# Two routed passes over 48 tiles each become one pass over 80 common tiles, with the shared units inside it

## The chip, the core and the metric

The kernel runs on one core of a Trainium2 chip. The metric is the device time of one execution in microseconds. The engines are PE (TensorE), DVE (VectorE), ACT (ScalarE), POOL (GpSimd) and SP (SyncE, which here only issues DMAs); each runs its own list of instructions in order and waits on semaphores that the others raise. The program writes every engine's list itself, so the order of the lists is the schedule.

## What is computed

Two batches of 1024 tokens with 256 features pass through two decoder layers. All but the last block (linear attention, two cross attentions, a spline block, causal attention) is untouched. The last block is a mixture of 16 experts, of which each token takes 4, plus one shared expert that every token takes:

```python
scores = jax.nn.sigmoid(x @ gate_w.T)                  # x: 2048 tokens x 256
topk_w, topk_ids = jax.lax.top_k(scores, K)            # K = 4 of E = 16
topk_w = topk_w / topk_w.sum(-1, keepdims=True)
comb = zeros((T, E)).at[arange(T)[:, None], topk_ids].add(topk_w)
g, u = einsum('th,ehi->tei', x, Wg), einsum('th,ehi->tei', x, Wu)
eo = einsum('tei,eih->teh', silu(g) * u, Wd)
routed = einsum('teh,te->th', eo, comb)
shared = silu(x @ sg) * (x @ su) @ sd
x = x + shared + routed
```

## The kernel before

Each token-expert pair (1024 x 4 per batch) gets a slot in a DRAM table of rows, `rows_by_slot`, one table per batch. Slots come in tiles of 128 rows, each tile of one expert only. An expert with n tokens takes n/128 tiles, rounded up; with 4096 pairs and 16 experts that can reach 48 tiles for one batch, and the program always works through all 48, whether they hold rows or not. Two tiles make a unit: 24 routed units per batch (`ROUTED_UNITS`), and 4 shared units of 2 tiles of tokens per batch. In all there are 56 units.

The steps of the last block, by batch b:

- `context_out(b, "e")`: 4 projections on PE (L720), each added to X by DVE (L1523) with the statistics of the layer norm behind it; then the norm and its transposes (L1408, L620).
- `route(b)`: gate scores on PE (L1006), then on DVE the choice of 4 experts (L1854 to L1877), each pair's place among its expert's rows from small matmuls on PE (L1015 to L1021), the number of tiles per expert and the first tile of each (L1893 to L1903), and each pair's slot (L1904 to L1917, which raises `slots_done`). POOL then waits for `slots_done` and issues the **dispatch**: 32 indirect DMAs (L2151), each of which scatters 128 rows into the table. DVE also works out the expert of each tile (L1921 to L1930, `experts_done`).
- `experts(b)`: a pipeline over units. In the turn of unit x, PE transposes the rows of unit x (L1041), multiplies those of unit x-1 by its experts' gate and up weights (L1055), transposes the hidden values of x-2 (L1067) and multiplies those of x-3 by the down weights (L1074). ACT copies and applies silu (L1353, L1358, L1366), DVE multiplies and copies (L1942, L1948), adds a shared unit's output to X (L1952), and for a routed unit finds the token of each row (L1960 to L1967). SP loads the rows of a unit (L2318) into one of 3 buffers; before the first unit of a batch it waits for all 32 dispatch DMAs of that batch.
- `results(b)`: POOL scatters each routed unit's output to `outs_by_token`, 2 indirect DMAs a unit (L2166), from 11 buffers.
- `combine(b)`: SP waits for all results of the batch and loads them back tile by tile (L2334, 512 KB each, 4 buffers for batch 0 and 8 for batch 1); DVE adds 4 weighted rows per token to X (L1981, 4 instructions a tile, 8 tiles). Stores of X follow (L2410).

`in_order` (L561) sets the order of all engines: every engine passes through the same nest of generators, and `next(other)` puts one step of a side job between two turns of the main job. Before the change `experts(0)` starts with the 4 shared units of batch 0 and then its 24 routed units, with `context_out(1, "e")` and `route(1)` beside it at two steps a turn; `experts(1)` starts with its routed units and ends with the 4 shared ones, with `combine(0)` beside it from turn 12. A turn's own work stands in the lists ahead of the side steps of the same turn.

## Time and profile before

| | us |
|---|---|
| median of 3 runs | 1254.06 |
| fastest, slowest of 3 | 1252.6, 1254.81 |
| span of the profiled execution | 1256.2 |
| PE busy | 1066.6 (85%) |
| DVE busy | 803.1 (64%) |
| ACT busy | 578.9 (46%) |
| POOL busy | 393.0 (31%) |

The profiled execution is 2.1 us longer than the median. Busy shares are averages over very different stages; the last block fills about the last 235 us, and what sets its pace has to be read there, from the timelines of its engines.

### The profile page before, as it was taken

The page shows a single profiled execution, that of the slowest core. Times are in us where ns is not written, and L with a number is a line of the kernel's source. Part 1 is how long each engine was busy: PE and PEld are TensorE (multiplying, and loading weights), DVE is VectorE, ACT ScalarE, POOL GpSimd, SP SyncE. Part 2 cuts the span into 40 slices and gives each one's busy share as a digit, 9 for nine tenths or more (in the row PEclk, how much of TensorE's full clock was granted, in tenths as well). Part 3 has the DMA queues.
Part 4 walks back from the last instruction along what each step waited for, and adds up shares of the span by engine and source line. Part 5 has one row for each costly group of instructions (what it writes and reads, how often), then busy time and mean ns, then how long its engine had stood idle before and what let it go on. Part 6 is the DMA issues. An engine that isn't in the chain of part 4 may idle for free.

```text
span 1256.2 us, 19418 instructions
## 1 busy us (share of the span) xinstructions
PE 1066.6 (85%) x6344; PEld 647.4 (52%) x6344; DVE 803.1 (64%) x2216; ACT 578.9 (46%) x1185; POOL 393.0 (31%) x458
## 2 busy tenths in 40 slices
PE   4688888997768885989999998988997888989993
PEld 2244554575534563324444453436555457878873
DVE  4867666658465558485577676717767954633576
ACT  2333026732367632367666554674443533434430
POOL 3231023320175430044100020003422730777771
PEclk9999889997679996599999999999997998999997
DMA  7145847672001460304133320007000211555665
GB/s 198 67 101 114 114 64 253 205 113 31 1 0 38 94 109 0 51 1 102 51 52 52 51 44 8 3 1 214 1 1 1 96 69 40 164 170 160 203 196 202
DMA packets 63201, 107.90 MB, mean 86 GB/s; under 512 B 13433, under 2 KB 35291, under 8 KB 62816
## 3 DMA queue, kind: packets, MB, share of 16 engines
q1 hardware_dynamic: 55104, 76.61, 27.6%
q0 software_dynamic: 7680, 17.07, 3.7%
q10 hardware_dynamic: 320, 12.98, 3.2%
q8 instruction: 55, 0.90, 0.3%
q14 instruction: 42, 0.34, 0.1%
HBM read 74.75 MB, written 48.89 MB: 98 GB/s over the span
## 4 chain that ended last, share of the span: by engine, by line
PE 52%; DVE 24%; ACT 8%; issue 7%; DMA 4%; POOL 3%; SPq 1%; DVEq 0%; ACTq 0%; POOLq 0%
PE psum L1055 7%; PE psum L934 5%; PE psum L720 4%; PE psum L904 4%; DVE mx L1796 4%; PE psum L956 4%; PE psum L1074 3%; PE psum L832 3%; PE psum L805 2%; PE psum L816 2%; DVE small L1581 2%; PE psum L620 2%; DVE work L1596 2%; PE psum L862 2%; DVE X L1981 1%
## 5 line engine op out<-in xcount | busy, mean ns | idle before, releaser
L1796 DVE TENSOR_REDUCE mx<-psum 128x1 f32<-128x512 f32 (+3 forms) x384 | 195.7, 551 | 89.5 <-PE psum L904 46.5
L1321 ACT ACTIVATE work<-psum 128x512 f32<-128x512 f32 (+1 forms) x192 | 92.5, 527 | 60.9 <-PE psum L959 41.0
L904 PE MATMUL psum<-stack_area 96*128 96x512 bf16 (+3 forms) x288 | 98.5, 353 | 25.1 <-DVE mx L1796 23.8
L2098 POOL TENSOR_TENSOR work<-work,small 128x308 f32<-128x308 f32 x107 | 74.7, 703 | 114.0 <-DVE small L1599 114.0
L805 PE MATMUL psum<-area 128*128 128x308 f32 x256 | 96.5, 461 | 14.2 <-DVE work L1596 11.5
L1321 ACT ACTIVATE HT<-psum 128x384 f32<-128x384 f32 (+2 forms) x192 | 81.1, 465 | 49.0 <-PE psum L959 31.6
L956 PE MATMUL psum<-stack_area 98*128 98x512 bf16 (+3 forms) x288 | 93.5, 337 | 7.9 <-ACT work L1321 2.8
L2006 POOL TENSOR_SCALAR rstd<-mv 128x4 f32<-128x4 f32 (+1 forms) x26 | 6.6, 255 | 298.2 <-DVE mv L1418 221.5
L1055 PE MATMUL psum<-area,work 128*128 x384 | 94.2, 390 | 5.7 <-ACT work L1353 5.7
L816 PE MATMUL psum<-const_tile,work 128*77 128x128 f32 x512 | 81.4, 285 | 15.1 <-ACT stack_area L1233 9.4
L1581 DVE TENSOR_REDUCE small<-psum 128x4 f32<-128x308 f32 x128 | 59.3, 463 | 51.9 <-PE psum L805 25.5
L816 PEld LDWEIGHTS psum<-const_tile,work 128*77 128x77 f32 x512 | 62.8, 152 | 52.8 <-POOL work L2098 31.0
L1942 DVE TENSOR_TENSOR work<-work,psum 128x256 f32<-128x256 f32 x56 | 23.5, 419 | 92.8 <-ACT work L1358 92.8
L620 PE MATMUL psum<-const_tile,H 128*128 128x128 f32 x224 | 44.0, 333 | 44.9 <-DVE H L1408 34.2
L1055 PEld LDWEIGHTS psum<-area,work 128*128 128x128 f32 x384 | 71.5, 196 | 14.5 <-issue 6.2
L1225 ACT ACTIVATE work<-work,rowany 128x308 f32<-128x308 f32 x64 | 35.3, 552 | 82.2 <-DVE work L1596 82.1
L904 PEld LDWEIGHTS psum<-stack_area 96*128 96x128 bf16 x288 | 28.7, 100 | 85.7 <-DVE mx L1796 47.0
L2166 POOL DMA_INDIRECT outs_by_token<-stack_area,area x66 | 65.4, 991 | 21.6 <-issue 18.6
L1233 ACT COPY stack_area<-psum 77x512 f32<-77x512 f32 x128 | 71.5, 566 | 1.3 <-PE psum L816 1.3
L2151 POOL DMA_INDIRECT rows_by_slot<-area x64 | 61.8, 965 | 22.1 <-issue 18.9
L805 PEld LDWEIGHTS psum<-area 128*128 128x128 f32 x256 | 42.3, 198 | 44.5 <-issue 21.8
L620 PEld LDWEIGHTS psum<-const_tile,H 128*128 128x128 f32 x224 | 30.4, 169 | 60.1 <-issue 28.7
(264 smaller groups left out, 2442.4 us busy)
## 6 DMA issues: line engine op xcount, KB each, us to landing
rows_by_slot<-in_unused_rows ACTq DMA_DIRECT2D x2, 6336.0 KB, 32.8
W<-rows_by_slot SPq DMA_DIRECT2D x48, 264.0 KB, 3.0
stack_area<-parts_a0q SPq DMA_DIRECT2D x24, 128.0 KB, 4.2
stack_area<-parts_a0k SPq DMA_DIRECT2D x24, 128.0 KB, 6.7
stack_area<-parts_a1q SPq DMA_DIRECT2D x24, 128.0 KB, 4.5
stack_area<-parts_a1k SPq DMA_DIRECT2D x24, 128.0 KB, 6.9
H<-outs_by_token SPq DMA_DIRECT2D x6, 512.0 KB, 4.1
area<-outs_by_token SPq DMA_DIRECT2D x6, 512.0 KB, 5.8
```

What stands on the lines that cost most here:

```text
L620: done = pe.transpose(u.bank(k)[:, q * P:(q + 1) * P], src[:, t, c * P:(c + 1) * P], ident)
L805: done = pe.matmul(s, queries[:, g // 2 if masked else g, t * P:(t + 1) * P], keys[:, g, :, :].rearrange("p j k -> p (j k)"), start=True, ...
L816: done = pe.transpose(turned.bank(i)[0:CTX, j * P:(j + 1) * P], work[i % 6][:, j * CTX:(j + 1) * CTX], ident)
L904: done = pe.matmul(u.bank(k)[:, 0:cols], stack["q"][0:KSTACK, j, t * P:(t + 1) * P], stack["k"][0:KSTACK, j, half * SPAN:half * SPAN + col ...
L956: done = pe.matmul(u.bank(k)[:, 0:cols], stack["k"][0:KSTACK + 2, j, kb * P:(kb + 1) * P], stack["q"][0:KSTACK + 2, j, c * SPAN + off:(c + ...
L1055: done = pe.matmul(u_g.bank(g)[:, q * D:(q + 1) * D], lhs, w, start=q == 0 and c == 0, stop=c == DC - 1, skip_group_check=True)
L1233: act.copy(pt[group % 2][0:CTX, :, q * P:(q + 1) * P], turned.bank(i)[0:CTX, :].rearrange("p (j n) -> p j n", j=HPG)).then_inc(*turned.emp ...
L1321: act.activation(p[:, 0:cols], u.bank(k)[:, 0:cols], ACT.Exp).then_inc(*u.empties(k))
L1581: dve.tensor_reduce(mx, s3, AX.X, ALU.max).then_inc(*steps.up())
L1796: dve.tensor_reduce(mxt[n % 2][:, j, t, half:half + 1], u.bank(k)[:, 0:cols], AX.X, ALU.max).then_inc(*u.empties(k))
L2098: pool.tensor_tensor(ex3, ex3, small[:, of_i + 4:of_i + 8].unsqueeze(2).to_broadcast([P, HPG, CTX]), ALU.mult).then_inc(ctx_prob, 1)
L2166: pool.indirect_dma_start(outs_dram[b], bass.IndirectOffsetOnAxis(m.out_row[:, tile:tile + 1], 0), unit_out[slot][:, q * D:(q + 1) * D], N ...
```

## The change

The tables of the two batches become one of 80 tiles (40 routed units). Batch 0 first gets the full tiles of each of its experts, rounded down instead of up. Then come 16 tiles, one for each expert, that take what is left of that expert from batch 0 and are filled up from batch 1; the rest of batch 1 follows. All engines now run one `experts()` of 48 units: 8 routed units (the first 16 tiles are always full tiles of batch 0), then the 8 shared units of both batches, then the other 32 routed units. SP waits for the dispatch of batch 0 before routed unit 0 and for that of batch 1 before routed unit 8. `combine(0)` now starts at turn 41 and needs the first 24 units' results; `combine(1)` needs all 40.

```diff
-DISPATCH_START, COMBINE_START, COMBINE_LAG = 13, 12, 2
+COMBINE_START, COMBINE_LAG = 41, 2
-ROUTED_UNITS = 24
+ROUTED_UNITS = 40
+EARLY_UNITS, FIRST_BATCH_UNITS = 8, 24
+ROUTE_RATES = (4, 2, 2, 2, 3, 3, 3, 3, 4)
+RESULT_RATES, RESULTS_FROM = {4: 1, 5: 1, 6: 1, 7: 1, 16: 2, 17: 2}, 20
...
             drain(other)
-            other, results = chain(e["context_out"](1, "e"), e["route"](1)), e["results"](0)
-            for n, _ in enumerate(e["experts"](0)):
-                next(other, None)
-                next(other, None)
-                if FIRST_ROUTED[0] + UNIT_STEPS <= n < DISPATCH_START:
-                    next(results, None)
-            drain(other)
-            results, other = chain(results, e["results"](1)), e["combine"](0)
-            for n, _ in enumerate(e["experts"](1)):
-                next(results, None)
-                if n % 2 == 0:
+            other, results, returned = chain(e["context_out"](1, "e"), e["route"](1)), e["results"](), e["combine"](0)
+            for n, _ in enumerate(e["experts"]()):
+                for _ in range(ROUTE_RATES[min(n, len(ROUTE_RATES) - 1)]):
+                    next(other, None)
+                for _ in range(RESULT_RATES.get(n, int(n >= RESULTS_FROM))):
                     next(results, None)
                 if n >= COMBINE_START:
-                    next(other, None)
+                    next(returned, None)
+            drain(other)
             drain(results)
-            drain(other)
+            drain(returned)
             drain(e["combine"](1))
...
# SP, experts
-                        if routed == 0:
-                            sp.wait_ge(dispatched[b].sem, 16 * TILES * TOPK)
+                        if routed == 0:
+                            sp.wait_ge(dispatched[0].sem, 16 * TILES * TOPK)
+                        if routed == EARLY_UNITS:
+                            sp.wait_ge(dispatched[1].sem, 16 * TILES * TOPK)
...
# DVE, route: the slots
-                dve.tensor_tensor(m.end, m.first, m.tiles, ALU.add).then_inc(*steps.up())
-                dve.scalar_tensor_tensor(m.slot, m.first.unsqueeze(1).to_broadcast([P, TILES, EXPERTS]), float(P),
-                                         u.bank(1)[:, 0:P].rearrange("p (t e) -> p t e", t=TILES), ALU.mult, ALU.add).then_inc(*u.empties(1))
+                if b == 0:
...
+                else:
+                    dve.tensor_tensor(m.end, m.first, m.tiles, ALU.add).then_inc(*steps.up())
+                    dve.tensor_scalar(m.base, const("iota16"), full_tiles, float(P), ALU.add, ALU.mult).then_inc(*steps.up())
+                    dve.tensor_scalar(m.bound, m0.left, -1.0, float(P), ALU.mult, ALU.add)
+                    dve.tensor_tensor(m.jump, m.first, const("iota16"), ALU.subtract).then_inc(*steps.up())
+                    dve.wait_ge(*steps.now())
+                    dve.tensor_tensor(m.base, m.base, m0.left, ALU.add)
+                    dve.tensor_scalar(m.end, m.end, full_tiles, float(EXPERTS), ALU.add, ALU.add)
+                    dve.tensor_scalar(m.jump, m.jump, float(EXPERTS - 1), float(P), ALU.add, ALU.mult).then_inc(*steps.up())
+                dve.wait_ge(*steps.now())
+                dve.tensor_tensor(m.past, place, m.bound.unsqueeze(1).to_broadcast(by_e), ALU.is_ge).then_inc(*steps.up())
+                dve.tensor_tensor(m.slot, place, m.base.unsqueeze(1).to_broadcast(by_e), ALU.add).then_inc(*u.empties(1))
+                dve.wait_ge(*steps.now())
+                dve.tensor_tensor(m.past, m.past, m.jump.unsqueeze(1).to_broadcast(by_e), ALU.mult).then_inc(*steps.up())
+                dve.wait_ge(*steps.now())
                 dve.wait_ge(*u.empty(1))
+                dve.tensor_tensor(m.slot, m.slot, m.past, ALU.add).then_inc(*steps.up())
...
# SP, combine
-                    sp.wait_ge(landing.sem, 16 * UNIT_TILES * results_in(slot, b))
+                    sp.wait_ge(landing.sem, 16 * UNIT_TILES * results_in(slot, ROUTED_UNITS if b else FIRST_BATCH_UNITS))
```

Where the lists change, line numbers of the changed kernel are some 10 to 55 higher: L1046 is the old L1041, L1063 L1055, L730 L720, L2206 L2151, L2220 L2166.

**POOL, around the dispatch of batch 1.** `rows_by_slot` rows are the dispatch, `outs_by_token` rows the results. Before:

```order
L2166 DMA outs_by_token<-work,area 4096x256 x6
L2166 DMA outs_by_token<-stack_area,area 4096x256 x2
L2151 DMA rows_by_slot<-area 6144x264 x2
L2166 DMA outs_by_token<-stack_area,area 4096x256 x2
L2151 DMA rows_by_slot<-area 6144x264 x2
L2166 DMA outs_by_token<-stack_area,area 4096x256 x2
L2151 DMA rows_by_slot<-area 6144x264 x28
L2166 DMA outs_by_token<-stack_area,area 4096x256 x10
```

and now:

```order
L2220 DMA outs_by_token<-work,area 8192x256 x6
L2220 DMA outs_by_token<-stack_area,area 8192x256 x2
L2206 DMA rows_by_slot<-area 10240x264 x32
L2220 DMA outs_by_token<-stack_area,area 8192x256 x14
L2220 DMA outs_by_token<-work,area 8192x256 x6
```

The first 8 result DMAs stay ahead of the dispatch, the 4 that stood inside it are behind it, and the dispatch is one row of 32.

**PE, the first turns of the experts' pipeline.** `bank` semaphores are those of PSUM, `unit0_landed` says that the rows of a routed unit are in SBUF. Before:

```order
L720 MATMUL psum<-W,H 128x256 [waits landed_wx,bank7_emptied,bank5_emptied,bank6_emptied,bank4_emptied,landed_moe]
L720 MATMUL psum<-W,H 128x256 x3
L720 MATMUL psum<-W,H 128x256 [waits bank7_emptied]
L720 MATMUL psum<-W,H 128x256 x3
L1055 MATMUL psum<-area,HT 128x256 [waits bank2_emptied]
L1055 MATMUL psum<-area,HT 128x256 x3
L720 MATMUL psum<-W,H 128x256 [waits bank7_emptied,bank4_emptied,bank5_emptied]
L720 MATMUL psum<-W,H 128x256 x3
L720 MATMUL psum<-W,H 128x256 [waits bank7_emptied]
L720 MATMUL psum<-W,H 128x256 x3
```

and now:

```order
L1046 MATMUL psum<-const_tile,W 128x128 [waits bank0_emptied,unit0_landed,landed_moe]
L1046 MATMUL psum<-const_tile,W 128x128 x3
L1069 TENSOR_LOAD area [waits experts_done]
L1069 ISA x2
L1069 TENSOR_LOAD area
L1069 ISA x2
L730 MATMUL psum<-W,H 128x256 [waits bank4_emptied,bank7_emptied,bank5_emptied,landed_wx]
L730 MATMUL psum<-W,H 128x256 x3
L730 MATMUL psum<-W,H 128x256 [waits bank7_emptied]
L730 MATMUL psum<-W,H 128x256 x3
L730 MATMUL psum<-W,H 128x256 [waits bank7_emptied,bank4_emptied,bank5_emptied]
L730 MATMUL psum<-W,H 128x256 x3
```

The transposes of routed unit 0 stand first, and the four projections of batch 1 (L730) follow in a block, all in one PSUM bank, where before a shared unit's products (L1055) stood between them.

**DVE, the slots of batch 1**, from the sum of an expert's first tile and its tiles to the product that spreads the slots. Before, down to `slots_done`:

```order
L1903 TENSOR_TENSOR area<-area 128x16
L1904 SCALAR_TENSOR_TENSOR area<-area,psum 128x128
L1907 TENSOR_TENSOR H<-area 128x512
L1910 TENSOR_REDUCE area<-H 128x32
L1912 CAST area<-area 128x32
L1914 TENSOR_SCALAR area<-area 128x32
L1915 TENSOR_SCALAR area<-area 128x32
L1917 SCALAR_TENSOR_TENSOR area<-area 128x32
```

and now, as far as that product (the six rows behind it are as before):

```order
L1925 TENSOR_TENSOR area<-area 128x16
L1926 TENSOR_SCALAR area<-const_tile,area 128x16
L1927 TENSOR_SCALAR area<-area 128x16
L1928 TENSOR_TENSOR area<-area,const_tile 128x16
L1930 TENSOR_TENSOR area<-area 128x16
L1931 TENSOR_SCALAR area<-area 128x16
L1932 TENSOR_SCALAR area<-area 128x16
L1934 TENSOR_TENSOR H<-psum,area 128x128
L1935 TENSOR_TENSOR area<-psum,area 128x128
L1937 TENSOR_TENSOR H<-H,area 128x128
L1940 TENSOR_TENSOR area<-area,H 128x128
L1942 TENSOR_TENSOR H<-area 128x512
```

Two rows ahead of the product have become eleven.

## Rows read from the trace of the kernel before

**Rows 1.** The page, chain of work that ended last, shares of the span

```profile
PE 52%; DVE 24%; ACT 8%; issue 7%; DMA 4%; POOL 3%; SPq 1%; DVEq 0%; ACTq 0%; POOLq 0%
```

**Rows 2.** Timeline of PE: start us, us, engine, line, operation, [idle before]

```profile
1021.67 1.99 PE L720 MATMUL psum<-W,H 128*128 128x256 f32 x8
1024.51 1.99 PE L720 MATMUL psum<-W,H 128*128 128x256 f32 x8 [0.85 <-DVE X L1523]
...
1050.06 5.25 PE L1006 MATMUL psum<-gate_weights,HT 128*128 128x16 f32 x32 [0.72 <-issue]
...
1073.74 0.60 PE L1041 MATMUL psum<-const_tile,W 128*128 128x128 f32 x4
...
1119.24 0.60 PE L1041 MATMUL psum<-const_tile,W 128*128 128x128 f32 x4
```

**Rows 3.** Timeline of PE, around its long wait

```profile
1128.84 3.78 PE L1055 MATMUL psum<-area,work 128*128 x8 [5.75 <-ACT work L1353]
...
1132.83 1.55 PE L1074 MATMUL psum<-stack_area,work 128*128 x4
```

**Rows 4.** Timeline of PE, last routed unit and last shared unit

```profile
1217.69 0.60 PE L1041 MATMUL psum<-const_tile,W 128*128 128x128 f32 x4
...
1220.94 1.89 PE L1055 MATMUL psum<-area,work 128*128 x8
...
1228.51 1.03 PE L1074 MATMUL psum<-stack_area,work 128*128 x4
...
1232.18 1.89 PE L1055 MATMUL psum<-area,HT 128*128 128x256 f32 x8
...
1235.67 1.89 PE L1074 MATMUL psum<-area,work 128*128 128x256 f32 x8
```

**Rows 5.** Timeline of POOL, dispatch of batch 0, then of batch 1

```profile
975.36 1.25 POOL L2151 DMA_INDIRECT rows_by_slot<-area  x1 [2.90 <-DVE area L1917]
...
1014.86 0.96 POOL L2151 DMA_INDIRECT rows_by_slot<-area  x1 [0.30 <-issue]
...
1078.13 0.96 POOL L2151 DMA_INDIRECT rows_by_slot<-area  x1 [0.30 <-issue]
...
1122.56 0.96 POOL L2151 DMA_INDIRECT rows_by_slot<-area  x1 [0.30 <-issue]
```

**Rows 6.** Timeline of DVE, route of batch 1: its first operation, and its slots

```profile
1061.69 0.22 DVE L1854 TENSOR_SCALAR area<-area 128x128 f32<-128x128 f32 x1
...
1071.39 0.28 DVE L1893 TENSOR_TENSOR H<-psum,const_tile 128x128 f32<-128x128 f32 x1
1071.71 0.29 DVE L1896 TENSOR_REDUCE area<-H 128x16 f32<-128x128 f32 x1
...
1076.97 0.19 DVE L1917 SCALAR_TENSOR_TENSOR area<-area 128x32 int32<-128x32 int32 x1
```

**Rows 7.** Timeline of SP, DMA issues: first rows loaded, first results returned

```profile
1018.15 154.88 SPq L2318 DMA_DIRECT2D W<-rows_by_slot  x37
...
1234.49 0.80 SPq L2334 DMA_DIRECT2D H<-outs_by_token  x2
```

**Rows 8.** DMA issues from 1017 to 1035 us: KB each, median us to landing

```profile
W<-rows_by_slot SPq DMA_DIRECT2D x3, 264.0 KB, 3.3
```

**Rows 9.** Busy us by stretch: PE PEld DVE ACT POOL, clock, DMA share, GB/s

```profile
974.40:1015.90 41.50, 36.31 (x183) 18.79 (x181) 38.89 (x113) 22.51 (x45) 31.03 (x32) 1.00 0.28 102
1078.10:1123.60 45.50, 44.99 (x250) 39.11 (x248) 20.26 (x85) 18.06 (x38) 34.72 (x36) 1.00 0.61 189
...
1053.00:1056.00 3.00, 3.00 (x15) 3.00 (x16) 0.00 (x0) 0.28 (x1) 0.00 (x0) 0.50 0.00 0
```

**Rows 10.** Waits from 1026 to 1256 us: total us, times, longest

```profile
PE psum L1041 <- DMA W<-rows_by_slot: 2.7, 4, 1.5
```

**Rows 11.** Timelines of POOL and DVE, last results and last combine

```profile
1232.21 0.97 POOL L2166 DMA_INDIRECT outs_by_token<-stack_area,area  x1 [0.30 <-issue]
...
1238.21 4.00 DVE L1981 SCALAR_TENSOR_TENSOR X<-H,area,X 128x256 f32<-128x256 f32 x8
```

More of the change, by code:

```diff
@@ L343, in routing_memory @@
             m.slot_tile = take(TILES * TOPK, I32)
-            m.slot_f, m.row_f = take(TILES * TOPK), take(ROUTED_UNITS * UNIT_TILES)
-            m.tiles, m.first, m.end = [take(EXPERTS) for _ in range(3)]
-            m.expert = take(ROUTED_UNITS * UNIT_TILES)
-            m.offset = take(ROUTED_UNITS * UNIT_TILES, I32)
-            m.out_row = take(ROUTED_UNITS * UNIT_TILES, I32)
+            m.slot_f = take(TILES * TOPK)
+            m.tiles, m.first, m.end, m.left, m.base, m.bound, m.jump = [take(EXPERTS) for _ in range(7)]
+            if b == 0:
+                m.expert, m.offset = take(ROUTED_TILES), take(ROUTED_TILES, I32)
+            else:
+                m.row_f, m.out_row = take(ROUTED_TILES), take(ROUTED_TILES, I32)
             m.is_k = take(TILES * TOPK * EXPERTS).rearrange("p (t k e) -> p t k e", t=TILES, k=TOPK)
@@ L1052, in experts @@
                                 else:
-                                    t = UNIT_TILES * (g - FIRST_SHARED[b]) + q
+                                    t = UNIT_TILES * pair + q
                                     lhs, w = HT[b][:, c, t * P:(t + 1) * P], wgu_shared[c]
-                                done = pe.matmul(u_g.bank(g)[:, q * D:(q + 1) * D], lhs, w, start=q == 0 and c == 0, stop=c == DC - 1,
+                                done = pe.matmul(u_gu.bank(g)[:, q * D:(q + 1) * D], lhs, w, start=q == 0 and c == 0, stop=c == DC - 1,
@@ L1351, in experts @@
                         if routed >= 2:
-                            act.wait_ge(*u_g.full(x - 2))
-                        act.copy(rows_t[routed % 2].rearrange("p s c n -> p (s c n)"), u_x.bank(routed)).then_inc(*u_x.empties(routed))
+                            act.wait_ge(*u_gu.full(unit_of(routed - 2)))
+                        act.copy(rows_t[routed % 2].rearrange("p s c n -> p (s c n)"), u_rows.bank(routed)).then_inc(*u_rows.empties(routed))
                     if 0 <= g < UNITS:
-                        act.wait_ge(*u_g.full(g))
+                        act.wait_ge(*u_gu.full(g))
@@ L1356, in experts @@
                         if g >= 2:
-                            act.wait_ge(*u_hidden[b].full(g - 2))
-                        act.activation(hidden[g % 2], u_g.bank(g).rearrange("p (s n) -> p s n", s=UNIT_TILES)[:, :, 0:INNER],
+                            act.wait_ge(*u_hidden.full(g - 2))
+                        act.activation(hidden[g % 2], u_gu.bank(g).rearrange("p (s n) -> p s n", s=UNIT_TILES)[:, :, 0:INNER],
                                        ACT.Silu).then_inc(silu_done, 1)
-                    if is_routed(b, d):
-                        routed = d - FIRST_ROUTED[b]
-                        slot, use = out_slot(b, routed)
-                        act.wait_ge(*u_d.full(d))
+                    if d >= 0 and (routed := routed_in(d)) is not None:
+                        slot, use = out_slot(routed)
+                        act.wait_ge(*u_down.full(d))
@@ L1907, in route @@
+                dve.wait_ge(*steps.now())
                 dve.tensor_tensor(m.of_k, m.is_k, m.slot.unsqueeze(2).to_broadcast(wide), ALU.mult).then_inc(*steps.up())
```

271 lines of the change are left out of this document (153 added, 118 removed).

## The prediction

> **What bounds the kernel now.** I read the chain that ended last first: 52% of the span is PE's own work and 24% DVE's [rows 1]. The change touches only the last block, so the timelines of its engines decide. PE is the pacemaker there. Between 1073.74 and 1119.24 us lie 14 routed turns, 3.25 us each [rows 2]; from 1220.94 to 1232.18 lie 4 turns without row transposes, 2.81 us each [rows 4]. The difference, 0.44, is one unit's row transposes. POOL is the second queue to watch: each indirect DMA takes 0.96 us and the next starts 0.3 later, so a dispatch of 32 takes 40.5 us from the first start (975.36) to the last end (1015.82), and every row of it has to be in DRAM before SP may load a unit [rows 5, 7]. Before, the dispatch of batch 1 (1078.13 to 1123.52) ran beside the 24 routed units of batch 0, so PE had work. It was longer than 40.5 only because 4 result DMAs stood in it. Its price was one wait of 5.75 us, since result buffers ran out behind it [rows 3].
>
> **The change, part by part.**
>
> *Units.* 56 turns become 48, all eight of them routed: 8 x 3.25 = 26.0 us less PE work. The number is fixed by the program, not by the data. The second start of the pipeline goes too. Whether this reaches the end depends on whether PE has work at every moment, so I walk through the new order.
>
> *Start.* The route of batch 0 gets longer on DVE: about eight more small operations at 0.19 us or less each, some of them side by side, and two more dependent ones on 128 columns, 0.28 us plus 0.04 [rows 6]: 1.8 us until its slots are done. Its tile table has 32 instead of 48 tiles, which gives some 0.7 back later, too late for the dispatch. DVE is the full engine there, 38.9 of 41.5 us busy [rows 9], so the context stage ends 1.1 to 1.8 later than 1021.67 [rows 2]. The dispatch of batch 0 ends 1.8 later as well; SP issued its first load 2.33 us after the dispatch ended, and the load takes 3.3 [rows 7, 8]: 1018.15 + 1.8 + 3.3 = 1023.3. That was covered by shared units before, and is now the first thing PE waits for. I take 1023.3, 1.6 later.
>
> *To the gate products.* By the end of L1006 at 1055.3 [rows 2], PE had done 5 products, 4 hidden transposes, 3 down products and 2 row transposes of units. In the new order it is 4, 3, 2 and 5. That is 3 x 0.44 more and 2.81 less, so 1.5 less. The four projections now stand in a block in one bank, and each waits 0.85 for DVE's sum [rows 2], one such wait more: +0.9. So the gate products end at 1055.3 + 1.6 - 1.5 + 0.9 = 1056.3. They ran partly at 1.2 GHz before (clock 0.50, [rows 9]); I leave that as it is.
>
> *To the slots of batch 1.* Before, DVE's first route operation came 6.4 us behind them (1061.69, [rows 6]), now without a shared unit's sum (0.6): 1062.1. From there to the end of L1917 it took 15.5 [rows 6], of which I count 4 turns of unit work at 1.5 and 0.4 idle, so 9.1 are the route's own. Now: own 9.1 + 1.8 = 10.9, 2 turns in between instead of 4 (three route steps a turn), 3.0. But the chain now meets PE twice. PE stands at the position matmuls until the choice is made, and DVE's next turn needs the product of a unit that stands behind them: 3.5 us, in which DVE has only 0.9 to do, so +2.6. PE waits some 4.5 us there, and may fall to 1.2 GHz again, which costs 0 to 2; I take 1. Slots done: 1062.1 + 10.9 + 3.0 + 2.6 + 1.0 = 1079.6, against 1077.2 before. The faster rates are eaten up by having fewer turns to hide in. Bounds: 1075 (no half clock, no meeting) and 1083.
>
> *To routed unit 8.* POOL starts 0.97 later (1076.97 + 0.19 to 1078.13, [rows 5, 6]), at 1080.6; its first 8 result DMAs are done by then. Dispatch 40.4, SP 2.33, load 3.3: the rows of unit 8 are there at **1126.6**. PE has only the end of units 6 and 7 and the 8 shared units meanwhile: from 1079.6 on about seven turns of 2.81, so it arrives at about 1099 and **waits 27 us**. This is where the 26 us go. In other words: the 8 shared units are worth 22.5 us, the dispatch with its landing 46.
>
> *From there to the last product.* After its 5.75 us wait, PE worked at 1.2 GHz: the product took 3.78 instead of 1.89, the down product 1.55 instead of 1.03 [rows 3, 4], 2.4 us in all. I take the same. Then 31 turns of 3.25 = 100.8 to the row transposes of the last unit, 3.25 to its product, and 5.4 from that to the end of the last down product (1232.18 to 1237.56, [rows 4]). `combine(0)` falls in the last ten turns; its 512 KB loads held PE's row transposes for 2.7 us in four waits [rows 10], which I take over (bounds 0 and 6, since DVE's 2 us per combined tile now also stands ahead of the last hidden copies). Last product: 1126.6 + 2.4 + 100.8 + 8.6 + 2.7 = 1241.1.
>
> *The tail.* Before, the last routed output left PE at 1229.54 (1228.51 + 1.03, [rows 4]), and four shared units covered what follows. Nothing does now: ACT's copy and the last two result DMAs 3.64 (to 1233.18, [rows 11]), SP's first load 1.31 (1234.49, [rows 7]), the load at most 3.72 (to 1238.21), four rows of 4.00 on DVE that follow 3.92 apart, 15.7 [rows 11], and 2.2 for the last store to the span's end at 1256.2. Together 26.6, against 18.6 from the last PE work to the end before: 8 us exposed. POOL's backlog, which ran to 1222 before, is gone but wasn't late at the end.
>
> *Sum*: 1241.1 + 26.6 = 1267.7, against 1256.2: +11.5. Taken over to the median, 1254.06 + 11.5 = **1265.6 us**.
>
> **A rule beside a row.** The dispatch of batch 0 was issued while DVE was 94% busy, that of batch 1 with DVE at 20.3 of 45.5 us [rows 9], and both go at the same 1.27 us per DMA [rows 5]. The new type casts and table operations of batch 1 stand right behind its slots, so beside the dispatch, some 3.3 us of DVE work in SBUF. If POOL stood still for all of it, the time would be 1269; that is a rival below. The Trainium skill ("SBUF — State Buffer", section "SBUF: two separate sides") says that POOL can't write the descriptors of a DMA that it issues while DVE makes a 32-bit copy inside SBUF, since both need one shared port. By that rule that rival would hold; the rows speak against it.
>
> **Rivals.**
> 1. *Not slower: the dispatch is covered.* If the rows of unit 8 land before PE asks for them, 27 and 2.4 us go: 1236. Every us that the slots come earlier is worth one us until then; it breaks even with before when the slots are done at 1068, 11.5 us earlier than I work out. For it: the route gets three steps a turn instead of two, and the removed work is real. Against it: the gate products end no earlier, the route's own DVE work alone is 10.9 us, and 1056.3 + 10.9 is already 1067. Full cover 3%, enough of it for faster 6%.
> 2. *No difference.* Slots at 1075, no half clock behind the long wait, no contention with `combine(0)`: 1267.7 - 4.6 - 2.4 - 2.7 = 1258, a median of 1256. 9%.
> 3. *Still slower.* Half clock in both waits, slots at 1083, and 6 us around `combine(0)`: 1267.7 + 3.4 + 3.3 = 1274, a median of 1272. 15%, the 1269 of POOL standing still (3%) among it.
> 4. *The forecast*, 1259 to 1270: 67%.
>
> **How the numbers follow.** A difference under 0.2%, 2.5 us, is no change. Faster 0.09, the same 0.09, slower 0.82. The range, 1255 to 1273, reaches from the lower bounds of the unknown terms to their upper ones, and leaves out most of rival 1 and the far end of rival 3.
>
> **What the profile would show.** PE's timeline has one idle stretch of 20 to 33 us ahead of an L1046, ended by the DMA of rows, just behind eight shared turns; SP's wait there names the dispatch. The first L2206 of batch 1 starts at 1077 to 1084 and the 32 of them take 40.4. Turns behind it are 3.25 us. The last product of PE ends 26 to 27 us ahead of the end. I am wrong if DVE finishes the slots ten us earlier than 1079.6, if the indirect DMAs go faster than 1.27 us each, or if the tail is much shorter than 26 us.

## The result, and the profile after

| | before | after |
|---|---|---|
| median | 1253.64 us, 4 runs | 1269.49 us, 4 runs |
| fastest, slowest | 1252.6, 1254.81 | 1267.27, 1276.06 |
| ratio, 95% interval | | 1.014, 1.0102 to 1.0178 |
| span of the profiled execution | 1256.2 | 1266.9 |
| PE busy | 1066.6 | 1038.8 |

The changed kernel is slower by 15.9 us in the medians, with 28 us less work on PE. The prediction was 1265.6, 11.5 slower.

PE, start us, us, operation and the idle time before it, from the first routed unit to the last product:

```profile
1017.70 0.66 PE L1046 MATMUL psum<-const_tile,W 128*128 128x128 f32 x4
1019.29 1.97 PE L730 MATMUL psum<-W,H 128*128 128x256 f32 x8 [0.94 <-ACT H L1248]
...
1052.63 3.62 PE L1063 MATMUL psum<-area,work 128*128 x8
...
1064.80 0.29 PE L1025 MATMUL psum<-area 128*128 128x128 bf16 x1 [3.94 <-DVE area L1881]
...
1066.41 3.62 PE L1063 MATMUL psum<-area,work 128*128 x8
...
1123.99 1.11 PE L1046 MATMUL psum<-const_tile,W 128*128 128x128 f32 x4 [25.80 <-DMA W<-rows_by_slot]
1124.90 3.61 PE L1063 MATMUL psum<-area,HT 128*128 128x256 f32 x8
...
1129.43 0.60 PE L1046 MATMUL psum<-const_tile,W 128*128 128x128 f32 x4
...
1132.68 0.60 PE L1046 MATMUL psum<-const_tile,W 128*128 128x128 f32 x4
...
1237.73 1.12 PE L1082 MATMUL psum<-stack_area,work 128*128 x4 [0.93 <-DVE work L2004]
```

The first row transposes start with hardly a pause behind the context stage: the rows of batch 0 landed at about 1017.5, just as PE got there. Between 1052 and 1070 two products take 3.62 us, twice the 1.89 of [rows 4]. The granted clock is at its lower level there, 1.2 GHz, behind the small matrices of the gate scores (from 1047.27) and behind the wait of 3.94 us, as windows over these two stretches show (columns as in [rows 9], the clock is the 0.50):

```profile
1050.00:1056.00 6.00, 6.00 (x21) 5.22 (x22) 0.00 (x0) 2.15 (x3) 0.00 (x0) 0.50 0.07 25
1065.00:1070.00 5.00, 5.00 (x29) 4.17 (x28) 0.35 (x2) 0.59 (x1) 0.00 (x0) 0.50 0.07 26
```

Then the row that decides: **25.80 us idle, ended by the DMA of rows**, and the turn behind it mostly at 1.2 GHz once more (5.44 us from 1123.99 to 1129.43 instead of 3.25). After that the turns stand 3.25 apart, as in [rows 2]. The chain of work that ended last shows the same in shares, against [rows 1]:

```profile
PE 49%; DVE 25%; ACT 8%; issue 8%; POOL 5%; DMA 4%; SPq 1%; DVEq 0%; POOLq 0%; ACTq 0%
```

PE went from 52% to 49%, POOL from 3% to 5%: the dispatch now lies on the path. POOL's timeline has both dispatches and the last results, to be laid beside [rows 5, 11]:

```profile
972.16 1.25 POOL L2206 DMA_INDIRECT rows_by_slot<-area  x1 [4.51 <-DVE area L1952]
...
1078.50 1.76 POOL L2206 DMA_INDIRECT rows_by_slot<-area  x1 [13.99 <-DVE area L1952]
1080.56 0.96 POOL L2206 DMA_INDIRECT rows_by_slot<-area  x1 [0.30 <-issue]
...
1118.50 0.96 POOL L2206 DMA_INDIRECT rows_by_slot<-area  x1 [0.30 <-issue]
...
1238.64 1.23 POOL L2220 DMA_INDIRECT outs_by_token<-stack_area,area  x1 [0.30 <-issue]
1240.18 1.13 POOL L2220 DMA_INDIRECT outs_by_token<-stack_area,area  x1 [0.30 <-issue]
1241.61 0.97 POOL L2220 DMA_INDIRECT outs_by_token<-stack_area,area  x1 [0.31 <-issue]
1242.89 0.97 POOL L2220 DMA_INDIRECT outs_by_token<-stack_area,area  x1 [0.30 <-issue]
```

The dispatch of batch 1 takes 41.0 us (1078.50 to 1119.46), one DMA every 1.27, and PE's wait ends 4.5 behind it. At the end four result DMAs stand close together, and the last is issued at 1243.86, 5.0 us after PE's last product (1238.85). DVE: the first route operation of batch 1, the hidden product that it waits for, the last operation of the slots, then combine(1):

```profile
1058.05 0.22 DVE L1858 TENSOR_SCALAR area<-area 128x128 f32<-128x128 f32 x1
...
1070.48 0.42 DVE L1998 TENSOR_TENSOR work<-work,psum 128x256 f32<-128x256 f32 x1 [5.10 <-ACT work L1363]
...
1077.53 0.19 DVE L1952 SCALAR_TENSOR_TENSOR area<-area 128x32 int32<-128x32 int32 x1
...
1248.88 4.01 DVE L2036 SCALAR_TENSOR_TENSOR X<-H,area,X 128x256 f32<-128x256 f32 x8 [7.38 <-DMA H<-outs_by_token]
...
1260.64 4.00 DVE L2036 SCALAR_TENSOR_TENSOR X<-W,area,X 128x256 f32<-128x256 f32 x8
```

SP, DMA issues, the first rows loaded and the first results of batch 1 returned, against [rows 7]:

```profile
1014.71 187.58 SPq L2370 DMA_DIRECT2D W<-rows_by_slot  x34
...
1245.38 0.80 SPq L2388 DMA_DIRECT2D H<-outs_by_token  x2
```

**Where the 15.9 us are.** The profiled spans differ by 10.7 only, and the reason lies ahead of the change. Windows of the kernel before in two stretches that it doesn't touch (columns as in [rows 9]):

```profile
240.00:360.00 120.00, 102.24 (x743) 68.23 (x736) 71.62 (x183) 48.62 (x95) 26.50 (x34) 0.83 0.29 49
360.00:600.00 240.00, 195.70 (x989) 103.87 (x988) 153.43 (x403) 131.32 (x272) 86.03 (x113) 0.86 0.27 53
```

and of the changed one:

```profile
240.00:360.00 120.00, 100.34 (x750) 67.42 (x750) 73.24 (x188) 53.27 (x102) 30.92 (x39) 0.89 0.29 49
360.00:600.00 240.00, 198.75 (x1008) 104.36 (x1008) 154.97 (x406) 131.02 (x273) 83.02 (x109) 0.86 0.28 55
```

In the first stretch the granted clock was 0.83 before and 0.89 after; in the second it was 0.86 in both. The last norm ahead of the dispatch of batch 0 started at 949.91 before and at 944.42 after, 5.5 us earlier. From that norm to the end it is 306.3 and 322.5 us, **16.2 more**, and that agrees with the medians. In all profiles of this study the first dispatch DMA starts somewhere from 966.6 to 978.2 (a last one, on another chip, apart), though no experiment edits anything ahead of it (the change itself puts a longer route of batch 0 there). So the experiments are read by the distance from that DMA to the end of the span, beside the medians: 280.8 us before, 294.7 after (plus 2.3 for the longer route ahead of it).

### The profile page after: what moved, and what is told of

It reads as the page before. It is cut to its first block, busy times and chain, and to the rows that moved or that the text cites. A ratio compares the mean times of both kernels' runs of the same rounds, so it can differ in the third digit from the quotient of the medians.

```text
span 1266.9 us, 18868 instructions
## 1 busy us (share of the span) xinstructions
PE 1038.8 (82%) x6200; PEld 623.9 (49%) x6200; DVE 796.0 (63%) x2191; ACT 567.1 (45%) x1161; POOL 378.0 (30%) x442
## 4 chain that ended last, share of the span: by engine, by line
PE 49%; DVE 25%; ACT 8%; issue 8%; POOL 5%; DMA 4%; SPq 1%; DVEq 0%; POOLq 0%; ACTq 0%
PE psum L1063 5%; PE psum L944 5%; PE psum L730 4%; PE psum L914 4%; DVE mx L1800 4%; PE psum L966 4%; PE psum L842 3%; PE psum L815 2%; POOL rows_by_slot L2206 2%; PE psum L826 2%; DVE small L1585 2%; PE psum L630 2%; PE psum L1082 2%; DVE work L1600 2%; DVE X L2036 1%
## 5 line engine op out<-in xcount | busy, mean ns | idle before, releaser
L1585 DVE TENSOR_REDUCE small<-psum 128x4 f32<-128x308 f32 x128 | 59.3, 463 | 51.1 <-PE psum L815 25.8
L1998 DVE TENSOR_TENSOR work<-work,psum 128x256 f32<-128x256 f32 x48 | 20.2, 421 | 109.0 <-ACT work L1363 109.0
L1063 PE MATMUL psum<-area,work 128*128 x320 | 79.2, 392 | 0.0
L2206 POOL DMA_INDIRECT rows_by_slot<-area x64 | 63.0, 984 | 37.4 <-issue 18.9
L2220 POOL DMA_INDIRECT outs_by_token<-stack_area,area x56 | 55.4, 989 | 41.8 <-ACT stack_area L1370 20.1
L1063 PEld LDWEIGHTS psum<-area,work 128*128 128x128 f32 x320 | 60.1, 198 | 7.1
L1600 DVE TENSOR_TENSOR work<-psum,small 128x308 f32<-128x308 f32 x128 | 60.0, 469 | 0.3
```

The costliest lines, as they stand in the source:

```text
L1063: done = pe.matmul(u_gu.bank(g)[:, q * D:(q + 1) * D], lhs, w, start=q == 0 and c == 0, stop=c == DC - 1, skip_group_check=True)
L1585: dve.tensor_reduce(mx, s3, AX.X, ALU.max).then_inc(*steps.up())
L1600: dve.tensor_tensor(ex3, s3, mx.unsqueeze(2).to_broadcast([P, HPG, CTX]), ALU.subtract).then_inc(*score.empties(n))
L2206: pool.indirect_dma_start(rows_dram, bass.IndirectOffsetOnAxis(m.slot_k[:, at:at + 1], 0), m.rows[:, t, :], None).then_inc(*dispatched[b]. ...
```

## The experiments

The theory: the dispatch of batch 1, which ran beside 24 routed units before, now runs beside eight shared ones, and the path to the end is route, dispatch, unit 8, 32 units, tail. The rival theories, named in the prediction or suggested by the result: the longer DVE route is the cause by itself; turns with less in them shift the dispatch; another queue (results, buffers, tables) is just as late; the tail is what costs.

| run | median us | ratio to before, 95% | PE's wait for rows of batch 1 | first dispatch DMA to end |
|---|---|---|---|---|
| before | 1253.3 to 1254.2 | | 0 | 280.8 |
| changed | 1269.49 | 1.014 (1.010 to 1.018) | 25.8 | 294.7 |
| changed, again | 1270.08 | 1.016 (1.009 to 1.022) | 25.5 | 296.0 |
| e1 half dispatch | 1249.01 | 0.997 (0.994 to 1.000) | 5.4 | 274.3 |
| e2 12 early units | 1254.59 | 1.004 (1.001 to 1.007) | 12.9 | 282.4 |
| e3 route first | 1248.12 | 0.996 (0.994 to 0.999) | 1.0 | 273.2 |
| e3 again | 1245.38 | 0.993 (0.990 to 0.996) | 1.3 | 274.0 |
| e4 shared split | 1269.97 | 1.014 (1.010 to 1.019) | 37.1 | 298.6 |
| e5 before, route first | 1257.71 | 1.005 (1.002 to 1.008) | 0 | 285.9 |
| e6 = e2 + e3 + e4 | 1240.15 | 0.989 (0.986 to 0.992) | 0 | 264.7 |
| e7 = e1 + e3 | 1246.91 | 0.995 (0.991 to 0.999) | 0 | 272.8 |
| e8 route in turn 4 | 1259.24 | 1.003 (1.001 to 1.006) | 13.0 | 281.9 |
| e9 e3, part of combine(1) on POOL | 1252.34 | 0.998 (0.996 to 1.001) | 1.3 | 276.6 |

**The changed kernel again.**

> The changed kernel itself again, beside the other three on the same chip, since its first runs lay between 1267.3 and 1276.1. My theory: 1268 to 1270, with 25.8 us of wait before unit 8 as in its first profile, since what varies lies in the stages ahead of the last block. Rival, the wait itself varies by several us with the time at which the dispatch lands: the end would vary with it.

1270.1, with the wait at 25.5. The two profiles of this one program differ by 4.4 us in when the first dispatch DMA starts (972.16 and 967.76), by 1.3 in what follows it, and by 0.3 in the wait. What varies lies ahead of the last block, as expected.

**Is the wait the dispatch?** Half of the DMAs of batch 1 are left out, and with them the rows of 512 tokens:

```diff
                 for t in range(TILES):
                     for k in range(TOPK):
+                        if b and t >= TILES // 2:
+                            yield
+                            continue
...
-                            sp.wait_ge(dispatched[1].sem, 16 * TILES * TOPK)
+                            sp.wait_ge(dispatched[1].sem, 16 * TILES * TOPK // 2)
...
-                    sp.dma_start(returned_rows[b][t % slots], by_token[t]).then_inc(*returned_landed[t % slots].up())
+                    sp.dma_start(returned_rows[b][t % slots], by_token[t % (TILES // 2) if b else t]).then_inc(*returned_landed[t % slots].up())
```

> The changed kernel, but only 16 of the 32 dispatch DMAs of batch 1 are issued (those of its first 512 tokens), and SP waits for 16. The rows of the other 512 tokens are left out, and combine(1) adds the routed sums of the first 512 tokens to them in their place; all turns, loads and results stay as many. My theory: the 25.8 us that PE stands before unit 8 are the dispatch, and nothing else is late there. 16 x 1.27 = 20.3 us less, so a wait of 5.5 us, and the end comes 20.3 us earlier, up to 22.7 if the half clock behind the wait goes too: a median of 1247 to 1249, against 1269.5 of the changed kernel. Rival A, something else is late behind the dispatch (results, buffers, tables of experts): the wait is replaced by another one and the gain is below 10 us, 1260 or more. Rival B, the time is in the longer route of DVE and not in the dispatch: hardly any gain.

The row transposes of unit 8, on PE:

```profile
1104.88 1.11 PE L1046 MATMUL psum<-const_tile,W 128*128 128x128 f32 x4 [5.43 <-DMA W<-rows_by_slot]
```

The median fell by 20.5, for 20.3 us of DMAs taken away. Nothing else was late behind the dispatch.

**Does work ahead of the wait cost anything?**

```diff
-EARLY_UNITS, FIRST_BATCH_UNITS = 8, 24
+EARLY_UNITS, FIRST_BATCH_UNITS = 12, 24
```

> The changed kernel with 12 early routed units instead of 8 (with this input batch 0 has 26 full tiles, so 24 tiles can go ahead; the program's guarantee is only 16). The same 48 turns, but four routed turns move from behind PE's long wait to ahead of it. My theory: the wait ends when the dispatch of batch 1 has landed, whatever PE does before; four turns of 3.25 us fill 13.0 of its 25.8 us, 12.8 remain, and the end comes 13.0 us earlier, 1256.5. Rival A, the turns only shift the dispatch (its route steps stand between turns, PE and DVE are full): wait and end stay within 3 us, 1267 or more. Rival B, the wait isn't a landing time but a chain through the results' buffers: then four more results ahead lengthen it, 1270 or more.

```profile
1119.26 1.12 PE L1046 MATMUL psum<-const_tile,W 128*128 128x128 f32 x4 [12.88 <-DMA W<-rows_by_slot]
```

Wait 12.9, as worked out, and the distance to the end 13 us shorter than the mean of the changed kernel's two profiles (295.4). Four turns moved into the gap were free. With rival A the dispatch would have moved; its first DMA comes 106.7 us after that of batch 0, 106.3 in the changed kernel.

**What is a turn inside the route worth?** e3 lists all side steps right behind the first turn, e8 lists those from the second half of the norm on in turn 4:

```diff
-ROUTE_RATES = (4, 2, 2, 2, 3, 3, 3, 3, 4)
+ROUTE_RATES = (64,)
```

```diff
-ROUTE_RATES = (4, 2, 2, 2, 3, 3, 3, 3, 4)
+ROUTE_RATES = (4, 2, 2, 2, 64)
```

> The changed kernel with all side steps (projections, norm and route of batch 1, dispatch issues) in the lists directly behind the first turn of the experts, not 4, 2, 2, 2, 3 ... a turn. No work is removed. My theory: the path is route, dispatch, unit 8, and turns that stand inside the route lengthen it one to one. Without them slots are done at about 1060 instead of 1077.7, the rows of unit 8 are there at about 1107 instead of 1123; the 7 other early turns and the 8 shared ones (45 to 48 us) just fill the 46 us of the dispatch, so the wait is under 3 us, and the end comes 15 to 18 us earlier: a median of 1252 to 1255. PE stands instead some 10 to 15 us in pieces inside the route, which costs nothing, as it is the path itself. Rival A, the idle time in the route is as dear as the wait it saves: 1266 or more. Rival B, more is won, since DVE and ACT finish the route faster than I count (slots before 1055): below 1250.

> The changed kernel with side steps 4, 2, 2, 2 in the first turns as it has them, and all others (the rest of the norm, gate products, route, dispatch) in turn 4, where it spreads them over turns 4 to 8 and beyond. It lies between the changed kernel (slots done 13.5 us... 19.7 us from the first route operation) and e3 (12.4 us). My theory: three unit turns leave the path (one ahead of the first route operation, two behind it). The first route operation comes 5.8 us earlier, as it no longer stands behind the turn after the gate products, and the slots 7.3 us more: 13 us earlier, the wait before unit 8 shrinks from 25.8 to about 13 us, and the time is 1270 - 13 = 1257. Rival, what e3 won lies in the first turns (projections and norm without unit work between them): then this is worth little, 1265 or more.

e3, DVE's first and last operation up to the slots, and PE's waits:

```profile
1045.56 0.23 DVE L1858 TENSOR_SCALAR area<-area 128x128 f32<-128x128 f32 x1 [12.01 <-ACT area L1348]
...
1057.74 0.19 DVE L1952 SCALAR_TENSOR_TENSOR area<-area 128x32 int32<-128x32 int32 x1
...
1051.11 0.29 PE L1025 MATMUL psum<-area 128*128 128x128 bf16 x1 [5.90 <-DVE area L1881]
...
1061.81 0.44 PE L1075 MATMUL psum<-const_tile,work 128*128 128x128 f32 x2 [3.52 <-DVE work L1998]
...
1103.65 0.66 PE L1046 MATMUL psum<-const_tile,W 128*128 128x128 f32 x4 [0.98 <-DMA W<-rows_by_slot]
```

The slots are done at 1057.93, 86.7 us after the first dispatch DMA (105.6 in the changed kernel), 12.4 us after the first route operation (19.7). PE stands 5.90 us inside the route, 3.52 right behind its slots, and 0.98 for the rows. The end comes 21.8 us earlier by the distance (mean of two profiles each): 19.4 from the earlier rows, the rest since the turn behind the wait now runs at full clock. Rival A, that idle time in the route is as dear, is out. e8 lies between, wait 12.99:

```profile
1113.09 1.11 PE L1046 MATMUL psum<-const_tile,W 128*128 128x128 f32 x4 [12.99 <-DMA W<-rows_by_slot]
```

Its time is 2.2 above the 1257 expected, its distance 13.5 under the changed kernel's. With the slots done 105.6, 92.8 and 86.7 us behind the first dispatch DMA (changed, e8, e3), the end is 295.4, 281.9 and 273.6 behind it: 12.7 us of route are 13.5 of time, and the next 6.1 are 8.3, with the half clock behind the wait, 2.2 us, gone at the last step. In this range a us of route is a us of time.

e3 ran a second time, as the pair of e9 (below):

> e3 itself again, as the pair of e9 on the same chip, and for a closer interval against the kernel before. My theory: 1248, a ratio of 0.996 as in its first runs. Rival: its first runs were lucky by some us, and it is the same as the kernel before, 1254.

1245.4 and 0.993 (0.990 to 0.996): the gain over the kernel before is real.

**Is route first simply better?** The same edit in the kernel before:

```diff
             for n, _ in enumerate(e["experts"](0)):
-                next(other, None)
-                next(other, None)
+                drain(other)
```

> The kernel before the change (two tables, 56 units), with the same edit as e3: all side steps of batch 1 directly behind the first turn. My theory: an earlier route is worth something only where PE waits for the dispatch. Here it never does, so 20 us earlier slots bring nothing; PE stands about 12 us more inside the route (17.7 us of gaps there in e3, 5.5 in the kernel before), with no wait later that it pays back, except the 5.75 us for result buffers and the 2.4 us of half clock behind it, which go since POOL has its dispatch done earlier. Sum +4: 1258. Rival A, route first is simply the better order: 1235 to 1245. Rival B, the gaps in the route are hidden by other work: 1246 to 1250.

1257.7: slower by 0.5%, by 5.1 us in the distance. Where routed units cover the dispatch, PE's gaps inside the route are paid and nothing is won.

**Is the dispatch dear where PE doesn't wait for it?** e3 with half a dispatch:

> e3 and e1 together: side steps first, and only 16 of the 32 dispatch DMAs of batch 1 (the rows of its last 512 tokens are left out, and the sums of the first 512 are added to them). My theory: in e3 PE is at the balance, 1 us of wait is left before unit 8, so 20 us less dispatch are worth 1 us: 1247. In e1 the same cut was worth 20.5 us. Rival, POOL's dispatch is dear in itself, also where PE doesn't wait for it (by the traffic or the late results): 1240 or less.

PE no longer waits for rows of batch 1 at all, yet the cut that was worth 20.5 us is now worth nothing clear of noise: 0.8 us by the distance, and a ratio of 0.995 that lies between the 0.996 and 0.993 of e3. The dispatch has no price of its own; e3 is at the balance, with 1.0 to 1.3 us of wait left.

**The tail against the wait.** Four shared units go behind the last routed one:

```diff
+        MIDDLE = SHARED_UNITS
...
-            return n - SHARED if EARLY_UNITS + SHARED <= n < UNITS else None
+            return n - MIDDLE if EARLY_UNITS + MIDDLE <= n < ROUTED_UNITS + MIDDLE else None
...
+            if ROUTED_UNITS + MIDDLE <= n < UNITS:
+                return divmod(n - ROUTED_UNITS, SHARED_UNITS)
...
```

> The changed kernel with the four shared units of batch 1 behind the last routed unit, where they stood before the change, and only the four of batch 0 in the middle. My theory: the four turns (11.2 us) come out of the cover of the dispatch, so PE waits 37.0 us instead of 25.8, and they cover the tail, which from PE's last down product shrinks from 28.05 to the 18.6 us of the kernel before, 9.4 less. Sum +1.8: 1271. Rival A, the tail isn't shortened (the results and the combine are late for another reason): +11.2, 1281. Rival B, the wait in the middle doesn't grow, since the dispatch starts earlier with less DVE and PE work ahead of it: 1260.

The first row is PE, the others are DVE in the tail, the last tiles of combine(0) and the first of combine(1):

```profile
1118.25 1.12 PE L1049 MATMUL psum<-const_tile,W 128*128 128x128 f32 x4 [37.10 <-DMA W<-rows_by_slot]
...
1245.21 2.04 DVE L2039 SCALAR_TENSOR_TENSOR X<-area,X 128x256 f32<-128x256 f32 x4
1247.17 4.00 DVE L2039 SCALAR_TENSOR_TENSOR X<-H,area,X 128x256 f32<-128x256 f32 x8
```

The wait grew by 11.3 to 37.1, and the time stayed: what the middle lost, the tail gave back. The distance is 3.2 longer, where 1.8 were expected; two profiles of one program differ by 1.3, so that excess says little. But the DVE rows show that the tail gave back less than it could: DVE goes from combine(0) to combine(1) without a gap, though POOL's last result DMA had been issued by 1236.88. In place of the results DVE itself is now late in the tail.

**All together.**

> The edits of e2, e3 and e4 together: 12 early units (for this input only), side steps first, four shared units in the middle and four at the end. My theory: PE has 12 routed and 4 shared turns, 50 us, for the 46 us from the slots to the rows of unit 12, so the wait stays near 0, as in e3, and now the four last shared turns cover 9.4 us of the tail: 1248.1 - 9.4 = 1238.7. Rival, the gains don't add, since the early units hold DVE or POOL up (results of 12 units behind the dispatch, 11 buffers): a new wait of 5 us or more behind the dispatch, 1244 or more.

1240.15, and 8.9 us under e3 by the distance, where 9.4 were expected. The gains add, since each fills another gap. It is faster than the kernel before by 13 us and than the changed one by 30, but it needs 24 full tiles in batch 0 (this input has 26; only 16 are sure). **e3 has no such condition and is faster than both kernels too**, 0.993 and 0.996 of the kernel before. In e6 DVE again has no gap between combine(0) and combine(1) (DVE rows), long after POOL's last result:

```profile
1221.53 2.04 DVE L2039 SCALAR_TENSOR_TENSOR X<-area,X 128x256 f32<-128x256 f32 x4
1223.48 4.00 DVE L2039 SCALAR_TENSOR_TENSOR X<-H,area,X 128x256 f32<-128x256 f32 x8
...
1212.24 0.98 POOL L2223 DMA_INDIRECT outs_by_token<-stack_area,area  x1 [0.30 <-issue]
```

So the last run moves combine(0) ahead:

```diff
-COMBINE_START, COMBINE_LAG = 41, 2
+COMBINE_START, COMBINE_LAG = 37, 2
```

> e6 (12 early units for this input, side steps first, four shared units at the end) with combine(0) from turn 37 instead of 41. In e6 DVE worked without a gap from its last eight tiles of combine(0) (2.04 us each, beside the shared units' sums) into combine(1): combine(1) began at 1223.48, though the last result DMA had been issued by 1213.22. My theory: there DVE has taken the place of the results as the bound of the tail. With combine(0) four turns earlier, combine(1) begins when its first rows are back: 1213.2 + 1.5 + 3.5 = 1218.2, 5.3 us earlier, and the time is 1240.2 - 5.3 = 1235. Rival A, turns with a combined tile are longer than 3.25 us whenever they come (SP's and DVE's steps stand in their way), so the four more of them among routed turns cost what the tail gains: 1239 to 1241. Rival B, SP then stands at the results of batch 0 ahead of row loads: slower than e6, 1243 or more.

It ran on another chip, on which the kernel before took 1324.99 us; this one took 1301.1, a ratio of 0.982 (0.977 to 0.986). The times can't be set beside the others: DVE and PE stood for 17 and 13 us inside the experts with nothing that they waited for in the profile, which no other run shows.

```profile
1119.52 0.42 DVE L2001 TENSOR_TENSOR work<-work,psum 128x256 f32<-128x256 f32 x1 [16.80 <-issue]
...
1125.29 0.66 PE L1078 MATMUL psum<-const_tile,work 128*128 128x128 f32 x2 [13.02 <-issue]
```

The tail can be read, though: POOL's last result, and the first of combine(1) on DVE.

```profile
1279.96 0.98 POOL L2223 DMA_INDIRECT outs_by_token<-stack_area,area  x1 [0.30 <-issue]
...
1286.18 4.01 DVE L2039 SCALAR_TENSOR_TENSOR X<-H,area,X 128x256 f32<-128x256 f32 x8 [0.32 <-DMA H<-outs_by_token]
```

From the end of the last result DMA's issue (1280.94) to the end it is 23.3 us, in e6 28.3 (1213.22 to 1241.5): 5.0 less, where 5.3 were expected. That this is 5 us of time on an undisturbed chip was not shown, nor what the earlier combine(0) costs among the routed turns (rival A), which can't be read there.

**DVE or the loads in the tail?** Two of the eight tiles of combine(1) go to POOL, in e3:

```diff
+POOL_TILES = (2, 5)
...
+                        pool.tensor_tensor(rows, rows, w.unsqueeze(2).to_broadcast([P, TOPK, D]), ALU.mult).then_inc(*steps.up())
...
+                        pool.tensor_tensor(rows[:, 0:2, :], rows[:, 0:2, :], rows[:, 2:4, :], ALU.add).then_inc(*steps.up())
...
+                        pool.tensor_tensor(rows[:, 0, :], rows[:, 0, :], rows[:, 1, :], ALU.add).then_inc(*steps.up())
...
+                        done = pool.tensor_tensor(X[:, b * TILES + t, :], X[:, b * TILES + t, :], rows[:, 0, :], ALU.add)
```

> e3 with two of the eight tiles of combine(1) (tiles 2 and 5) on POOL instead of DVE: one product of 128x1024, one sum of 128x512 and two of 128x256 a tile, with their own semaphore. My theory: in the tail DVE is the bound, 15.7 us for eight tiles in a row without gaps. Six tiles take 11.8; POOL's share is about 2.4 + 1.2 + 0.65 + 0.65 = 4.9 us a tile (by 1.15 to 1.26 us for 128x512), ready with both by some 2 to 3 us before DVE's old end. The time falls by 2.5 to 3.9 us: 1244.9. Rival A, the loads are the bound in the tail (4 MB in 13 us): no gain, 1248. Rival B, POOL and DVE slow each other in SBUF: DVE's 0.49 us a row grows and the gain is below 1 us, or a loss.

Slower than its pair: 0.998 (0.996 to 1.001) against 0.993 (0.990 to 0.996) of the kernel before, and 276.6 against 274.0 us by the distance. This was a miss. DVE's six tiles now take 18.2 us (1231.19 to 1249.42), where eight had taken 15.7:

```profile
1231.19 5.51 DVE L2041 SCALAR_TENSOR_TENSOR X<-H,area,X 128x256 f32<-128x256 f32 x8 [7.58 <-DMA H<-outs_by_token]
...
1245.42 4.00 DVE L2041 SCALAR_TENSOR_TENSOR X<-W,area,X 128x256 f32<-128x256 f32 x8
```

The groups of DVE and POOL in the tail show why (count, busy us, mean ns, idle before):

```profile
L2041 DVE SCALAR_TENSOR_TENSOR X<-area,X 128x256 f32<-128x256 f32 x4 | 5.1, 1282 | 0.1
L2041 DVE SCALAR_TENSOR_TENSOR X<-W,area,X 128x256 f32<-128x256 f32 x8 | 3.8, 484 | 0.2
...
L2236 POOL TENSOR_TENSOR area<-area 128x1024 f32<-128x1024 f32 x1 | 2.1, 2090 | 8.3 <-DMA area<-outs_by_token 8.3
L2236 POOL TENSOR_TENSOR HT<-HT,area 128x1024 f32<-128x1024 f32 x1 | 2.1, 2069 | 0.0
```

DVE's operation takes 484 ns with POOL idle and 1282 on average in the tile that lay wholly beside POOL's work, one of them 1996, about the length of POOL's product (2090). It is rival B. The rule of the Trainium skill ("SBUF — State Buffer", section "SBUF: two separate sides") that a DVE instruction with two SBUF inputs and a POOL instruction that reads SBUF hold one port pair in turn, each for its whole length, agrees with these rows.

## Why the prediction was right, and where its terms were off

The time, 1269.5, lies in the range of 1255 to 1273, 3.9 above the forecast. The mechanism was the one forecast; the terms, set out from the first dispatch DMA of batch 0 where the stages ahead differ:

- **Units, 26.0 us less.** Right. From the rows of unit 8 to the end of the last down product it is 114.9 us (1123.99 to 1238.85), worked out as 114.5. The pace of 3.25 held to the turn of 1220.43. combine(0) cost 3.3 us instead of 2.7, and by another way than was put down: its loads held the row transposes for 1.4 us, and DVE's sums, standing ahead of the last hidden copies, held PE for most of the rest (0.78 and 0.93). The prediction had named that second way only in its bounds.
- **Start.** The longer route of batch 0 cost 2.3 us, not 1.8: norm to first dispatch DMA 27.7 against 25.5. PE's first row transposes came 45.5 us behind that DMA, 46.1 expected. The wait for them that was forecast did not come: PE left the context stage as the rows landed.
- **Slots of batch 1: the step that was off most.** From the first route operation to the slots it took 19.7 us, forecast 17.5. Two terms were too small. The route's own work was put at 10.9; e3, which has nothing between, shows 12.4, 0.3 of it a wait for the position matmuls. I had taken four unit turns at 1.5 us out of the profile before, and they were shorter (the two in the changed kernel 1.3 each). And the meeting with PE was put at 2.6 with 1.0 for the half clock; DVE stood 5.10 us for the hidden product. The half clock was there, on a product of 3.62 us that stood between DVE and its next operation. With a first route operation 1.0 us later, the slots were done 105.6 us behind the first dispatch DMA, where 102.4 were worked out: as late as the prediction's upper bound for them, 1083, which is 105.8 behind.
- **To unit 8.** The dispatch took 41.0 (40.4 expected; its first DMA 1.76 instead of 0.96), and the rows came 4.5 us behind it instead of 5.6.
- **The wait.** PE came to it 4 us later than worked out (126.0 behind the first dispatch DMA, not 121.8), held up with the slots, and the rows 2.4 later: 25.8 us instead of 27. The wait came out near its forecast because two errors of one sign, from the late slots, cancel in it; and the rows were only 2.4 late because the shorter landing took back 1.1 of the 3.5 us by which the dispatch ended late. e1, e2, e3 and e8 show that this wait is the path. The half clock behind it cost 2.2 us against 2.4.
- **The tail.** 28.05 against 26.6. The result DMAs took 5.0 instead of 3.6 behind the last product, since the unit before had come late through ACT and PE (DVE's combine(0) stood ahead of the last hidden copy, 0.93 us) and its two DMAs stood in front. These two took 1.23 and 1.13 us, beside DVE's combine(0), and the two behind them 0.97 each. Return load, DVE's 15.7 and the store were as taken over.
- Together the terms give 0.5 (start) + 2.8 (rows of unit 8 2.4 later, 0.4 more from there to the last product) + 1.4 (tail) = 4.7 us more than 11.5, which is the 16.2 measured from norm to end.

**Rival 1**, the dispatch is covered, did not happen, and e3 shows that it was within reach of one line. Breaking even was put at slots done at 1068, 90.8 us behind the first dispatch DMA as forecast: e8, with 92.8, came out at 1.003 of the kernel before and e3, with 86.7, at 0.993 and 0.996. **Rival 2** needed the half clock and combine(0) to cost nothing; the first cost 2.2 us and the second 3.3. **Rival 3** had, as one part, POOL standing still for all 3.3 us of DVE's work in SBUF behind the slots. That did not come: DVE's cast at 1080.85 lay within a dispatch DMA of 0.96 us (the one at 1081.55 fell between two DMAs and says nothing), and the whole dispatch was 0.5 us longer than the 40.5 of [rows 5]. But it was not free either: the first DMA took 1.76 us, 0.8 more than the next, beside the table operations of DVE.

That the changed kernel is slower was thus right for the reason given, shown by e1 and e2 on the wait, e3 and e8 on the route, e4 on the tail, e5 and e7 on the reverse.

## What to carry to other kernels

Before work is cut from a loop, ask what runs beside it: here 24 routed units had been the cover of a dispatch that takes 46 us with its landing, and the common table leaves eight shared ones there, 22.5 us, since routed unit 8 may hold rows of batch 1. What the cut units saved was spent again on the wait, and the half clock behind it and the bare tail came on top. Where an engine waits at the end of such a chain, put the chain's steps ahead of all filler on every engine, even if engines stand idle inside it; where it is covered, the same order costs. And when a filler is moved from one gap to another, ask which engine is next in the new place.

## What was new on the hardware

- An indirect DMA of 128 rows took POOL 0.96 us, and the next started 0.30 later; 32 in a row took 40.3 to 41.0 us in every run. It is the price of this dispatch.
- DVE's work did lengthen single ones: the first DMA of batch 1 took 1.76 us in the changed kernel, beside table operations of DVE, and result DMAs that lay within DVE's combine(0) up to 1.23 us instead of 0.97 (1238.64). Which kind of operation does it, and by what, no run here separates.
- DVE and POOL elementwise work side by side in SBUF: 484 ns became 1282 on average in one tile. Moving a quarter of a DVE-bound tail to an idle POOL made it longer.
- PE's clock fell to its lower level behind waits much shorter than the long one: the product behind waits of 3.94 and 25.80 us (changed kernel) and of 3.52 us (e3) took 3.6 us instead of 1.89, where the product ahead of the wait had taken 1.89; behind one of 2.67 us (changed kernel, 1078.53) it took 1.89. In e3 the one behind 5.90 us took 3.40, but there the clock had been low since the gate scores (0.50 from 1038 to 1045). So such a wait cost PE its length and up to 2.2 us more (the turn of 5.44 instead of 3.25).
- Stages that no edit touched reached the first dispatch DMA up to 11.6 us apart in the thirteen profiles, the one on the other chip left out; the granted clock between 240 and 360 us was 0.83 in two of them, the one of before and the latest (e7, 978.21), and 0.87 to 0.90 in the others. A difference of a few us in one profiled span has to be read behind a common landmark.
